# Typed-message stage of a graph kernel: the one-hot tile becomes TensorE's weights, and the gathered rows are weighted and moved as two fp32r parts

## The reference

```python
def _L1_gnn_ref(h, weight, norm, src, dst, rel_type):
    transformed = jnp.einsum('ni,rio->rno', h, weight)     # 16 types
    msg = transformed[rel_type, src] * norm                # one weight per edge
    out = jax.ops.segment_sum(msg, dst, num_segments=h.shape[0])
    return out
```

## Time and profile before

| | us |
|---|---|
| median of 3 runs | 4361.2 |
| span of the profiled execution | 4602.8 |
| typed-message stage in it, first gather to last window sum | 2429.0 to 3595.6 |
| GpSimd gathers of the stage | 784, 751.2 us busy |
| TensorE busy in the window 2428 to 3600 | 745.8 of 1172 |
| VectorE busy there | 294.1 |
| ScalarE busy there | 17.7 |
| TensorE's granted clock there | 0.57 of full |

### The profile page before, as it was taken

One profiled execution on the slowest core, in us unless ns is written; L12 is line 12 of the kernel. 1 busy time (PEld: TensorE's weight loads), 2 busy tenths in 40 slices (PEclk: granted clock), 3 DMA queues, 4 the chain that ended last, 5 costly groups with the idle time before them and its releaser, 6 DMA issues. The chain is left out here.

```text
span 4602.8 us, 88005 instructions
## 1 busy us (share of the span) xinstructions
PE 3885.9 (84%) x23733; PEld 3489.0 (76%) x23733; DVE 2976.4 (65%) x7006; ACT 2107.0 (46%) x4811; POOL 2125.1 (46%) x2102
## 2 busy tenths in 40 slices
PE   7899999999999988989995666667666699999993
PEld 6798898989889877987885655556556578888883
DVE  7698898989889876554332222222321488989888
ACT  3565565656556536763221000000000288989882
POOL 0455555555555501000006666666666167667671
PEclk9899999999999987999995555665655599999996
DMA  4466666656556610004443333333333123323225
GB/s 138 135 176 171 171 175 171 177 170 175 169 170 177 169 31 23 24 26 161 151 150 103 89 87 89 92 87 91 87 89 90 52 55 75 63 67 70 60 48 120
DMA packets 226998, 509.09 MB, mean 111 GB/s; under 512 B 51805, under 2 KB 94299, under 8 KB 220426
## 3 DMA queue, kind: packets, MB, share of 16 engines
q0 software_dynamic: 116736, 313.66, 24.7%
q1 hardware_dynamic: 106389, 187.30, 14.6%
q10 hardware_dynamic: 3679, 5.79, 0.4%
HBM read 434.08 MB, written 72.49 MB: 110 GB/s over the span
## 5 line engine op out<-in xcount | busy, mean ns | idle before, releaser
L685 POOL DMA_INDIRECT big<-table,e_idx x784 | 751.2, 958 | 1049.6 <-DVE e_idx L721 649.0
L356 POOL DMA_INDIRECT big<-table,e_idx x784 | 767.0, 978 | 856.9 <-issue 304.1
L703 PE MATMUL psum<-e_near_hot,big 128*128 128x64 f32 x3136 | 621.9, 371 | 377.6 <-issue 361.9
L703 PEld LDWEIGHTS psum<-e_near_hot,big 128*128 128x128 f32 x3136 | 616.7, 292 | 391.7 <-issue 386.7
L2191 POOL DMA_INDIRECT g_S<-gsrc,g_idx x512 | 588.8, 1150 | 274.8 <-issue 157.8
L748 DVE TENSOR_TENSOR big<-big,psum 128x128 f32 x196 | 56.6, 289 | 801.9 <-remote 489.6
L435 ACT ACTIVATE e_hT_hi<-psum 128x256 fp32r<-128x256 f32 x784 | 300.2, 383 | 593.9 <-PE psum L375 513.1
L468 DVE TENSOR_TENSOR big<-psum,big 128x512 f32<-128x512 f32 x784 | 539.4, 688 | 45.5 <-issue 22.8
L386 PE MATMUL psum<-e_w_hi,e_hT_hi 128*128 128x256 f32 x1568 | 509.8, 325 | 0.3 <-issue 0.3
L386 PE MATMUL psum<-e_w_hi,e_hT_lo 128*128 128x256 f32 x1568 | 443.7, 283 | 0.0
L386 PE MATMUL psum<-e_w_lo,e_hT_hi 128*128 128x256 f32 x1568 | 440.7, 281 | 0.0
(11 more groups left out here) (397 smaller groups left out, 9090.5 us busy)
## 6 DMA issues: line engine op xcount, KB each, us to landing
big<-in_attr_t SPq DMA_DIRECT2D x392, 128.0 KB
g_rest<-gpart SPq DMA_DIRECT2D x128, 256.0 KB
big<-table,e_idx POOLq DMA_INDIRECT x1568
table<-C SPq DMA_DIRECT2D x26, 896.0 KB
table<-n_rows SPq DMA_DIRECT2D x24, 896.0 KB
experts<-g_region SPq DMA_DIRECT2D x15, 560.0 KB
g_S<-gsrc,g_idx POOLq DMA_INDIRECT x512
table<-big SPq DMA_DIRECT2D x25, 224.0 KB
```

The costliest lines, as they stand in the source:

```text
L356: pool.indirect_dma_start(G[:, j % 2, q, :], None, table, bass.IndirectOffsetOnAxis(idx[:, j, q:q + 1], 0)).then_inc(s[f"G_in{j % 2}{q}"], 16)
L685: pool.indirect_dma_start(G[:, j % n, q, :], None, c.table1, bass.IndirectOffsetOnAxis(idx[:, j, q:q + 1], 0)).then_inc(s[f"G_in{j % n}"], 16)
L703: last = pe.matmul(acc[:, b, :], G[:, j % n, q, b * 128:(b + 1) * 128], onehot[:, q, :], start=q == 0 and (b == 0 or s is sems[1]), stop=q ...
```

## The change

`Attention` gets its two weight matrices as views of free space in `big`, and its `Exp` becomes a step (`ACT_STEPS`) within ScalarE's loop. The first pass of `stage_relations` is rewritten, and the second keeps its old form under the names `far_*`. For each sup:

- GpSimd fetches the same rows, but waits for `low` of seven sups ago rather than for `sup_done`.
- ScalarE makes `hi`, the rows times their edge weight, rounded to fp32r: four activations with a scale per partition. It also copies the sum of two sups ago out of PSUM (`evict`).
- VectorE makes `lo`, the weighted row less `hi`, with four scalar_tensor_tensor instructions, first in its step. The one-hot tile is one comparison, with no multiplication. The window sum comes last in the step and two sups late.
- TensorE loads the one-hot tile (64 columns, fp32r) and moves `hi` and `lo` (256 columns each): 8 fp32r matmuls. The sum has nodes on the partitions, so two transposes through the identity turn it for `agg`.

```diff
-    NEAR_SLOTS, FAR_SLOTS, ACCS = 7, 2, 4
-    LEAD = 4
+    SLOTS, HOTS, FAR_SLOTS, FAR_BANKS = 7, 4, 2, 4
+    LEAD = 2
...
+        hi, lo = (sb(n, [128, 2, SUP, D], F32R) for n in ("hi", "lo"))
+        near_hot = sb("near_hot", [128, HOTS, SUP, WIN], F32R)
+        rows = c.C[0:WIN, 0:2, :]
...
+        def near_pool(pool):
...
-                    pool.wait_ge(s["sup_done"], p * NSUP + sup + 1 + NEAR_SLOTS - n)
+                    pool.wait_ge(s["low"], sup + 1)
...
+        def near_scalar(act):
+            def high(a):
+                k, j, sup = a
+                act.wait_ge(G_in[j % SLOTS], (k * (SUPS // SLOTS) + j // SLOTS + 1) * 16 * SUP)
+                act.wait_ge(s["sup_done"], sup + HOTS - 1)
...
+                for q in range(SUP):
+                    last = act.activation(hi[:, j % 2, q, :], G[:, j % SLOTS, q, :], ACT.Identity, scale=scale[:, j, q:q + 1])
+                last.then_inc(s["high"], 1)
+            def evict(a):
+                k, j, sup = a
+                act.wait_ge(s["sup_done"], sup + HOTS + 1)
+                act.wait_ge(s["turned"], sup + 1)
+                act.activation(rows[:, j % 2, :], acc(j), ACT.Copy).then_inc(s["rows"], 1)
...
-                for q in range(SUP):
-                    for b in range(KB):
-                        last = pe.matmul(acc[:, b, :], G[:, j % n, q, b * 128:(b + 1) * 128], onehot[:, q, :],
-                                         start=q == 0 and (b == 0 or s is sems[1]), stop=q == SUP - 1, skip_group_check=True)
+                pe.wait_ge(s["hot_ready"], sup + 1)
+                pe.wait_ge(s["low"], sup + SLOTS + 1)
+                pe.wait_ge(s["rows"], sup + 1)
+                for q in range(SUP):
+                    for n, part in enumerate((hi, lo)):
+                        last = pe.matmul(acc(j), near_hot[:, j % HOTS, q, :], part[:, j % 2, q, :],
+                                         start=q == 0 and n == 0, stop=q == SUP - 1 and n == 1)
...
+            def turn(a):
+                k, j, sup = a
+                pe.wait_ge(s["rows"], sup + 3)
+                pe.wait_ge(s["added"], sup + 1)
...
+                for b in range(KB):
+                    last = pe.transpose(turned(j)[:, b, :], rows[:, j % 2, b * 128:(b + 1) * 128], c.ident[0:WIN, 0:WIN])
+                last.then_inc(s["turned"], 1)
...
-                dve.tensor_tensor(made, made, bc(norm[:, at_sup], 2, width), ALU.mult).then_inc(s["hot_ready"], 1)
+            def low(a):
+                k, j, sup = a
+                dve.wait_ge(s["high"], sup + 1)
+                for q in range(SUP):
+                    last = dve.scalar_tensor_tensor(out=lo[:, j % 2, q, :], in0=G[:, j % SLOTS, q, :], scalar=scale[:, j, q:q + 1],
+                                                    in1=hi[:, j % 2, q, :].bitcast(F32), op0=ALU.mult, op1=ALU.subtract)
+                last.then_inc(s["low"], 1)
...
+            def step(k, v, beside=None):
+                if at(k, v):
+                    low(at(k, v))
+                if at(k, v + LEAD):
+                    hots(at(k, v + LEAD))
+                b = at(k, v - 2)
+                if b:
+                    add_window(b)
```

More of the change, by code:

```diff
@@ L217, in on_tensor, with on_scalar @@
             last.then_inc(self.out_ready, 1)
[L219 to L223, removed]
+    def on_scalar(self, act, g, h):
+        n = HALVES[h][1]
+        act.wait_ge(self.low_ready, g * 2 + h + 1)
+        act.activation(self.low[:, :, 0:n], self.low[:, :, 0:n], ACT.Exp).then_inc(self.exp_ready, 1)
     def on_vector(self, dve, step, g, h, before):
@@ L644, in at @@
+        G_in = [c.sem(f"{tag}G_in{j}_0") for j in range(SLOTS)]
+        f = {n: c.sem(f"{tag}{n}_1") for n in ("idx_ready", "hot_made", "hot_ready", "sup_done", "added", "shifted")}
+        far_in = [c.sem(f"{tag}G_in{j}_1") for j in range(FAR_SLOTS)]
+        begun_adding, begun_gathering, begun_turning = (c.sem(tag + "begun_" + n) for n in ("adding", "gathering", "turning"))
         def at(k, v):
@@ L649, in at, with far_loop, near_loop, acc @@
             return k, v, k * SUPS + v
[L651 to L676, removed]
+        def far_loop(eng, step, first):
+            for v in range(first, SUPS):
+                step(0, v)
+            with eng.Fori(1, NB - 1) as k:
+                for v in range(SUPS):
+                    step(k, v)
+            for v in range(SUPS + 1):
+                step(NB - 1, v)
+        def near_loop(eng, step, first, after, aside):
+            for v in range(first, SUPS):
+                step(0, v)
+            with eng.Fori(0, NT // GROUP) as g:
+                for v in range(SUPS):
+                    step(g + 1, v, lambda: aside(v % TURN, g, v // TURN, (g + 1) * SUPS + v))
+            for v in range(SUPS + after):
+                step(NB - 1, v)
+        def acc(j):
+            return c.ps[4 + j % 2][0:WIN, 0:D]
+        def turned(j):
+            return c.ps[6 + j % 2][:, 0:KB * WIN].rearrange("p (b n) -> p b n", b=KB)
+        def near_pool(pool):
             with pool.Fori(0, NB) as k:
@@ new lines, in far_acc, with far_pool @@
+        def far_acc():
+            return c.psum[:, 6:6 + KB, 0:FAR_WIN]
+        def far_pool(pool, p):
+            with pool.Fori(0, NB) as k:
+                for j in range(SUPS):
+                    sup = k * SUPS + j
+                    if j % TURN == 0:
+                        pool.wait_ge(f["idx_ready"], p * (2 * NB) + k * 2 + j // TURN + 1)
+                    pool.wait_ge(f["sup_done"], p * NSUP + sup + 1)
+                    pool.sem_inc(begun_gathering, 1)
+                    for q in range(SUP):
+                        pool.indirect_dma_start(G[:, j % FAR_SLOTS, q, :], None, c.table1,
+                                                bass.IndirectOffsetOnAxis(idx[:, j, q:q + 1], 0)).then_inc(far_in[j % FAR_SLOTS], 16)
@@ L762, in step, with far_passes @@
                     indices(a[0] + 1, 0)
[L763 to L764 removed]
             indices(0, 0)
             indices(0, 1)
[L768 to L782 removed]
+            far_loop(dve, step, -1)
+            dve.wait_ge(f["added"], (p + 1) * NSUP + FAR_BANKS)
+            dve.tensor_scalar(rel[:, :], rel[:, :], -float(FAR_WIN), None, ALU.add).then_inc(f["shifted"], 1)
+            dve.wait_ge(f["shifted"], p + 1)
+        def far_passes(eng, one):
             more = eng.value_load(far_i[0:1, 0:1], min_val=0, max_val=1)
```

210 lines of the change are left out of this document (126 added, 84 removed).

## The result

The changed kernel takes 4384.3 us (median, 4380.3 to 4387.6), the kernel before 4361.6 (4360.7 to 4364.4) beside it: a ratio of 1.0053, 95% interval 1.0039 to 1.0068, or 22.7 us more. In its profile the span is 4382.4 us, so this execution is one like the others; that of before was 4602.8.

The account below looks back on a forecast made before the run. GpSimd's gather issue was taken to bound the typed-message stage, at about 972 us in runs. +45 for `low`, -9 for the multiplication L734 removed and +2 for the tail gave +38 us, 4399 us, range 4347 to 4520.

Parts of the forecast that it names:

- The stage of a run stands at GpSimd's floor: Typed-message stage: in runs, unlike the profile, GpSimd's gather issue already sets the time, about 972 us.
- The 972: Typed-message stage: 1150.8 us from first to last gather less 178.6 us of pauses, taken as GpSimd's floor.
- The 241.6 us "do not exist in a run": Whole kernel: profile span 4602.8 less runs' 4361.2 us; 178.6 us taken as typed-message-stage pauses mostly belonging to the profiled execution.
- The 63 us left unplaced: Whole kernel: the rest of the 241.6 us after the 178.6 us of gather pauses, given no place.
- Rival 1: Typed-message stage: TensorE's slow passages exist in runs too, so the change removes pauses: -141 us, 4220 us; chance 0.14.
- TensorE, ScalarE and VectorE are covered: Typed-message stage: their changed work stays hidden beside the gathers, ScalarE at 417 and VectorE at 536 of 972 us.
- GpSimd's gathers get longer by the port, one `low` at a time: Typed-message stage: each `low` singly holds up gathers through the port VectorE and GpSimd share, +45 us; forecast's chance 0.54.
- The law of the square of the length: Gathers beside two-input VectorE instructions: each costs about 0.26 times its squared length in us, from L734, L474 and L2576.
- Rival 3: Typed-message stage: a sup's four `low` hold the port as one, +141 to +167, -7: 4495 to 4521 us; chance 0.10.
- +2 for the tail: End of the typed-message stage: only the last sup's longer chain is exposed, +2 us.
- +45 - 9: Typed-message stage gathers: +45 us for `low` holding them, -9 us for the multiplication L734 that goes.
- 4399: Whole kernel: the forecast time in us, +38 us against the median of 4361.2; chance 0.54.

Follow-up runs that it names:

- e1: The kernel before, run again unchanged as a second kernel: 4359.3 us, ratio 1.0001.
- e10: The changed kernel without its low part, plus a fifth ScalarE Identity per sup ahead of the four: 4348.3 us, 0.9971 of the kernel before.
- e2: The changed kernel without its low part (no `low` on VectorE, no second product on TensorE): 4367.1 us, 1.0014 of the kernel before.
- e8: The changed kernel with each `low` as two instructions of 128x128, on the slower chip: 4714.9 us, 1.0234 of the kernel before.
- e6: The changed kernel with its one-hot in four one-input tensor_scalar of 128x64 per sup, on the slower chip: 4717.3 us, 1.0252 of the kernel before.
- e12: The complete changed kernel plus one ScalarE Identity of 128x320 per sup ahead of the four high parts: 4410.6 us, 1.0110 of the kernel before.

## Where the prediction was right and where it was wrong

- **The stage of a run stands at GpSimd's floor**: right. e1 has 985.0 us from first to last gather. The 972 took off whole pauses with the 0.30 us that each gap has anyway; what exceeds 0.30 us is 162.3 us, which leaves 988.5.
- **The 241.6 us "do not exist in a run"**: true of the runs of the result, false as it was put. They exist in every run of another chip. The 63 us left unplaced were the other stages: in e1, the same program, the typed-message stage starts 38.8 us earlier and what follows its gathers is 40.7 us shorter, 79.5 us together. Rival 1 asked the right question and had the wrong sign: where the stalls are real, two kernels built like the changed one lose more (1.023 and 1.025) and the one without a low part 1.003; none gains them. The changed kernel itself was not run there.
- **TensorE, ScalarE and VectorE are covered**: right. 523, 405 and 517 of 1025 us. `hi` took 496 ns, not 407, and `low` 479, not 416; ScalarE's 80 us of copies were 71.
- **GpSimd's gathers get longer by the port, one `low` at a time**: the mechanism is right, and the steps on its price failed twice. First, L730 was said to cost nothing. It holds as L734 does; the pair of the earlier trace rows showed two phases, and I read two kinds of instruction. With it the comparison of the changed kernel, L766, stood in the sum at nothing, and it cost 15.6 us. The Trainium skill ("SBUF — State Buffer", section "SBUF: two separate sides") says that whichever starts first gets the shared pair for the whole instruction. The trace agrees with that but for the 0.06 us above, and with its two SBUF inputs for L730 (ten gathers held by it in e1 waited 103 to 247 ns); by the exception that it makes, only against a GpSimd operation that reads SBUF, neither line would matter unless issuing a gather counts as one, and here gathers are held. Whether it is their reading that is held no run shows. Second, `low` was put at 45 us, 57 ns each, and cost 18.1, 23 ns each. Held gathers cost 33.7 us in the changed kernel against 10.1 in the profile before, 5.5 in e1: +24 or +28 net, where +45 - 9 stood.
- **The law of the square of the length**: not borne out, and that its three points agreed was luck as far as the traces tell. The first was misread: with L730 counted the 10.1 us belong to 392 instructions, 26 ns each, or 0.14 in place of 0.26, and 14 ns each in e1. The second and third are no averages over all phases: in the trace of before 161 of 195 L474 start 1.0 to 1.375 us behind a gather's start, just ahead of the next one (190 gathers started beside one, 138 ns each), and 82 of 124 L2576 start 0.25 to 0.5 us behind one. `low` starts in step with the gathers too, so its price is that of its phase: for the comparison alone between 0 (e10) and 96 ns (e2: 18.8 us / 196), where the square gives 45.
- **Rival 3**: one gather over 1.5 us at 256 columns in the changed kernel, 40 at 128 columns (e8).
- **+2 for the tail**: not seen by itself; the span outside the gathers is 2.2 us shorter than in e1, inside the scatter of 14 us.

So 4399 was 15 us too high, and the time fell into the range partly by luck: the price of `low` was 2.5 times too large (45 us for 18.1), and the comparison behind it, put at nothing, made up for 15.6 of these 27 us. e6, which replaces that comparison, bears this out: its gathers took 973 ns in place of 988.

## What to carry to other kernels

Where GpSimd's own instructions pace a stage, every long VectorE instruction from SBUF beside them can have a price, though VectorE is half idle, and the price hangs on the phase: read the start of both in the timeline, over a few periods, before blaming a line. If one engine is released by what the other started, the phase is locked, and adding 0.4 us to the chain may win (e10) or lose (e12), so try the shift before cutting work. And when the span of a profile and the runs differ by 5%, ask on which chip each was taken before calling the difference the profiler's.

## What the runs showed of the hardware that I had not expected

- A gather of 128 rows takes 946 ns undisturbed (975 at most in e10, 784 of them), and 0.30 us lie between two. It is held only at one moment, about 0.1 us into it; an instruction of VectorE that starts after a wait and behind the gather's start costs it nothing (170 in e10).
- Back-to-back instructions 0.40 us apart let GpSimd in at the next boundary, as a rule (20 of 784 gathers in e12 took over 1.5 us); those 0.27 us apart (128 columns) often did not: 40 gathers over 1.5 us in e8, up to 2.73 us for one.
- A tensor_scalar from SBUF to SBUF in fp32 (354 ns for 128x256) holds gathers too, for what is left of it.
- The same program took 4360 us on one chip and 4606 on another, with the clock at 0.875 and 0.855; on the slower one GpSimd pauses for 3.69 us and ScalarE for 16.55 us (e6) with nothing in the trace that explains it.
